# Expert products of the older multiplication, moved ahead of two of four spread batches on TensorE

## What is computed

```python
x = x + _L0_conv_ref(_ln_c(x), conv_w, conv_b)      # conv over [max, mean] of channels, sigmoid, x * scale
t = _to_tokens(x)
router_probs = softmax(ln(t) @ router_w + router_b)
top_p, top_i = top_k(router_probs, 2); top_p /= sum(top_p)
expert_out = einsum('bnd,edc->bnec', ln(t), expert_w) + expert_b
t = t + einsum('bnk,bnkc->bnc', top_p, gathered)     # gathered: expert_out at top_i
```

## Time and profile before

| | us |
|---|---|
| median of 3 runs (lowest, highest) | 1424.98 (1424.57, 1428.08) |
| the profiled execution, its own time | 1424.37 |
| its span in the trace | 1422.6 |
| PE busy | 1310.0 (92%) |
| DVE busy | 1240.8 (87%) |
| POOL busy | 1069.4 (75%) |
| ACT busy | 1054.4 (74%) |

### The profile page before, as it was taken

One profiled execution on the slowest core, in us unless ns is written; L12 is line 12 of the kernel. 1 busy time (PEld: TensorE's weight loads), 2 busy tenths in 40 slices (PEclk: granted clock), 3 DMA queues, 4 the chain that ended last, 5 costly groups with the idle time before them and its releaser, 6 DMA issues.

```text
span 1422.6 us, 33089 instructions
## 1 busy us (share of the span) xinstructions
PE 1310.0 (92%) x11750; PEld 616.6 (43%) x11750; DVE 1240.8 (87%) x1527; ACT 1054.4 (74%) x3949; POOL 1069.4 (75%) x643
## 2 busy tenths in 40 slices
PE   8954999999999999999999999999999988899998
PEld 8853444444444444444444444444444322333332
DVE  5786799979999899988999899988999889987776
ACT  6567898888988898888988899888897334444442
POOL 5334787887788787887887887887888886887765
PEclk9955999999999999999999999999999999999999
DMA  6442466666667667676666666576665555566663
GB/s 220 121 124 81 133 205 195 195 195 203 203 187 219 190 209 211 174 224 195 195 182 216 190 209 204 175 231 198 200 197 156 156 156 156 156 178 185 175 189 117
DMA packets 85845, 259.97 MB, mean 183 GB/s; under 512 B 13744, under 2 KB 13744, under 8 KB 85680
## 3 DMA queue, kind: packets, MB, share of 16 engines
q1 hardware_dynamic: 85680, 257.85, 60.6%
HBM read 206.42 MB, written 51.38 MB: 181 GB/s over the span
## 4 chain that ended last, share of the span: by engine, by line
PE 53%; DVE 24%; issue 12%; POOL 2%; ACT 1%; DVEq 0%; POOLq 0%; ACTq 0%
PE moe L561 31%; DVE gx L703 15%; PE gb L507 8%; PE tm L486 8%; PE tm L500 2%; DVE ge L725 2%; PE moe L555 2%; DVE stats L680 2%; PE tm L546 1%; DVE ot L716 1%; DVE oh L738 1%; PE tm L585 1%; DVE u L788 1%; POOL dl L1235 1%; DVE early_s L680 0%
## 5 line engine op out<-in xcount | busy, mean ns | idle before, releaser
L561 PE MATMUL moe<-gx,wc 128*64 128x448 f32 x3584 | 813.4, 554 | 0.0
L703 DVE TENSOR_TENSOR gx<-gb,xd 128x896 f32<-128x896 f32 x672 | 707.3, 1085 | 85.6 <-PE gb L507 84.8
L1175 POOL TENSOR_TENSOR gx<-gs,xd 128x896 f32<-128x896 f32 x224 | 494.1, 2206 | 250.8 <-ACT gs L990 195.8
L990 ACT ACTIVATE gs<-gb 128x896 f32<-128x896 f32 x224 | 205.3, 916 | 193.9 <-PE gb L507 188.5
L952 ACT ACTIVATE sq<-xct 112x64 f32<-112x64 f32 x1400 | 338.4, 246 | 7.8 <-DVE early_s L690 2.1
L561 PEld LDWEIGHTS moe<-gx,wc 128*64 128x64 f32 x3584 | 217.9, 136 | 195.0 <-issue 162.0
L952 ACT ACTIVATION_READ_ACCUMULATOR sq<-xct 112x1 f32 x1400 | 265.4, 190 | 0.0
L507 PE MATMUL gb<-s,cg 32*128 32x448 f16 x1792 | 186.6, 360 | 64.5 <-DVE gx L703 63.3
L1192 POOL TENSOR_TENSOR tt<-xc,a1s 128x896 f32<-128x896 f32 x112 | 235.5, 2103 | 11.4 <-issue 9.7
L507 PEld LDWEIGHTS gb<-s,cg 32*128 32x128 f16 x1792 | 51.0, 91 | 402.5 <-DVE gx L703 336.4
L486 PE MATMUL tm<-rhs,xa 64*112 64x74 f32 x2800 | 184.6, 272 | 11.8 <-ACT logit_mean L937 8.4
(11 more groups left out here) (93 smaller groups left out, 1091.7 us busy)
## 6 DMA issues: line engine op xcount, KB each, us to landing
xd<-in_x_dram SPq DMA_DIRECT2D x448, 224.0 KB, 4.1
xa<-in_x_dram SPq DMA_DIRECT2D x112, 448.0 KB, 4.5
xc<-in_x_dram SPq DMA_DIRECT2D x112, 448.0 KB, 4.7
out_dram<-ot SPq DMA_DIRECT2D x112, 448.0 KB, 3.6
gx<-in_const_g_dram SPq DMA_DIRECT2D x1, 384.0 KB, 4.7
cf<-in_const_f_dram SPq DMA_DIRECT2D x1, 333.5 KB, 2.8
cf<-in_L_ffn_expert_b_dram SPq DMA_DIRECT2D x12, 1.0 KB
gx<-in_L_ffn_expert_w_dram SPq DMA_DIRECT2D x1, 128.0 KB, 4.5
```

What stands on the lines that cost most here:

```text
L561: last = pe.matmul(moe[b * CH:(b + 1) * CH, c, 0:HALF], wc[:, k * CH:(k + 1) * CH], gx[:, u, b, :], start=False, stop=(k == KT - 1), skip_ ...
L703: dve.tensor_tensor(gx[:, i, :, :], gb[:, 2 * slot:2 * slot + 2, 0:HALF], xd[:, v % 2, :, c * HALF:(c + 1) * HALF], ALU.mult).then_inc(sca ...
L990: act.activation(gs[:, j, :, :], gb[:, 2:4, 0:HALF], ACT.Copy).then_inc(gate_out, 1)
L1175: pool.tensor_tensor(gx[:, ND + j, :, :], gs[:, j, :, :], xd[:, v % 2, :, j * HALF:(j + 1) * HALF], ALU.mult).then_inc(scaled_p, 1)
```

## The change

It moves two calls on PE's queue. In batch 1, E5 of the step before now stands ahead of S1 and SP1, and in batch 3, E2 stands ahead of S4, SP0 and the convolution. No instruction is added or dropped, every wait stays with its instruction, and no other engine's program is changed.

```diff
@@ -605,11 +605,11 @@
                     v = step - LAG
                     cur, ahead = on(r, v), on(r, v + 1)
 
+                    if on(r, v - 1):
+                        experts_of_dve(r, v - 1, 5)
                     if cur:
                         spread_for_dve(r, v, 1)
                         spread_for_pool(r, v, 1)
-                    if on(r, v - 1):
-                        experts_of_dve(r, v - 1, 5)
                     if ahead:
                         turn(r, step, v + 1)
                     if cur:
@@ -626,13 +626,12 @@
                         experts_of_pool(r, v, 0)
 
                     if cur:
+                        experts_of_dve(r, v, 2)
                         spread_for_dve(r, v, 4)
                     if ahead:
                         spread_for_pool(r, v + 1, 0)
                     if Bp and step == 2:
                         convolve(r, A)
-                    if cur:
-                        experts_of_dve(r, v, 2)
                     if ahead:
                         spread_a1(r, step, v + 1, A, Bp)
                     if cur:
```

## The result

The changed kernel takes 1488.31 us, median of 4 runs (1485.12 to 1489.38), beside 1424.81 us for the kernel before: a ratio of 1.0436, 95% interval 1.0413 to 1.0459. It is 63.5 us slower.

A forecast was written before the change was run, and what follows sets the result against it. It took PE's order and whatever holds PE up as the bound beside pass A. The profiled 1424.37 us, plus 80 there, minus 31 afterwards, gave 1473, or 1474 as median; own range 1450 to 1495, stated range 1432 to 1495.

The forecast's parts named there:

- the first stretch: Where pass A runs beside pass C: later spreads stall PE, 13.6 us a round, +80 us in all.
- two chains on ACT: Copies behind the gate copy: s late by 0.80 us, a1 by 0.38, each delaying PE's centring in batches 2 and 4.
- The light step: Step beside pass A with PE busy throughout: 10.92 us, claimed to become 12.10 by stalls of 0.80 and 0.38.
- the sigmoid's 0.7: Step 2: with E2 no longer between convolution and A1, A1 waits some 0.7 us for the sigmoid and handovers.
- The eleven ordinary steps: Steps of a round other than step 2 and the two heavy ones: average 11.25 us, claimed to become 12.17.
- DVE's cover: Batch 1: DVE's gate work or remaining time before S2 hides the 0.80 us later spread, at no cost.
- Rival (1): Only batch 2's stall counts, in the eleven ordinary steps: 52 us less 31, 1445 us; chance 0.13.
- Pass C alone: Last stretch: moved products fill PE's holes, a step falls from 10.23 to 8.96 us; 15 steps, -19 us.
- round 8: Stretch with router work but no pass A: a gain between 0 and 18 us, taken as 12.
- the trap: Router comparison L725 took 7.19 us beside gapless POOL work; its time may shift, left unchanged with 11 us either side.
- the page's version: By the exclusive DVE and GpSimd port lock, shorter steps leave fewer gaps: the stretch without pass A gains 20 us, not 31.
- rival (3): DVE and POOL block each other in more steps, or loads come late in short steps: 1500 us; chance 0.05.

The follow-up runs named there:

- E5: Not a run: PE's expert product call for unit 5, moved in batch 1; against the kernel before, moving only it took 1473.13 us, ratio 1.0335.
- E2 behind the convolution: Changed kernel, but in step 2 E2 stands in its old place after the convolution; 1475.4 us, the middle of two runs.
- the new order from round 8 on: Kernel before, with both moves made only in rounds without pass A; 1413.27 us, ratio 0.9919.
- batch 3 alone: Kernel before, with only E2 moved ahead of S4, SP0 and the convolution, E5 left in place; 1436.02 us, ratio 1.0070.
- the kernels with waits: Three POOL waits for DVE in round 8, added to changed kernel, kernel before, and the new order from round 8 on; 1478.00, 1423.40 and 1406.14 us.
- the copy of parts moved: Changed kernel, with ACT's copy of parts placed after its copy of s instead of ahead of it; 1474.06 us.

## Why the prediction came out as it did

**The mechanism in the first stretch held, step by step.** The claim was that PE's sum doesn't change, that spreads 0.80 later cost DVE nothing, and that two chains on ACT end 0.80 and 0.38 later. Measured were stalls of 0.76 and 0.30, in those two places, 0.14 us behind the ends of those two copies, each shown alone by its own run and the first also from ACT's side. The light step was given as 12.10 and is 11.99; step 2 as 14.9 and is 14.79, with the sigmoid's 0.7 confirmed as 0.68; the heavy steps as +1.0 and are +0.7 (12.93). The eleven ordinary steps average (173.68 - 2 x 12.93 - 14.79) / 11 = 12.09, given as 12.17. A round costs 12.1 where 13.6 was forecast, and the stretch 74.7 where it was 80.

**DVE's cover was as thin as said.** In the light step S2 waits for nothing, so "that last quarter of a microsecond" was enough. Rival (1), that only the stall in batch 2 counts, fell: the one in batch 4 stands in the light step with 0.30, and alone in its own run. DVE's waits absorb a part, as the sum had it: the average ordinary step rose by 0.84 of the 1.07 us.

**Pass C alone**: 8.96 forecast, 8.91 measured, PE busy for all of it. The merged products, the spread behind them, and the window of the step:

```profile
1383.72 2.48 PE L561 MATMUL moe<-gx,wc 128*64 128x448 f32 x12
...
1386.13 0.37 PE L507 MATMUL gb<-s,cg 32*128 32x448 f16 x4
...
1386.43 0.58 PE L500 MATMUL tm<-cg,parts 112*64 112x112 f16 x16
...
1386.43:1395.34 8.91, 8.91 (x78) 3.17 (x74) 7.42 (x8) 4.11 (x5) 7.33 (x5) 1.00 0.73 207
```

The twelve records are E4, EP1 and E5 together, and the transposes follow the full spread of batch 1 by 0.30. That no load would be late in the shorter step, which was only taken to be so, was right: nothing waited there.

**The term that was wrong is round 8.** "Between 0 and 14 x 1.27 = 18, I take 12" was the gain; it was a loss of 9.0. The prediction named the trap, kept the price as it was in the earlier trace rows, and left 11 us either way. It was 21 off. What failed is "I leave it as it is": the blocked instructions became three (24.0 us together, where they need 1.1, 1.1 and 0.6) where one took 7.19 and two were stretched to 2.15 and 2.88, and PE's idle time behind them brought the lower clock three times on twelve records, where it came twice on eight. Why they became more is argued and not shown: POOL has the same work in these 14 steps before and after, 127 to 130 us, while a step in which nothing is blocked can shrink from 10.24 to 8.91 us, which should leave fewer gaps; no run changed that alone. Part of it is chance: the third instruction took 7.83 us here, but 4.79 and 4.81 in two runs whose round 8 is the same (E2 behind the convolution, and the new order from round 8 on). The sentence on the Trainium skill there (SBUF — State Buffer, section "SBUF: two separate sides", an exclusive lock on a shared port pair held for the whole instruction) pointed the right way, and the version of the sum by it, 20 us of gain in the drained stretch where 31 was taken, came nearer to the measured 8. The runs agree with the lock: a DVE instruction with two operands in SBUF comes down to its own time, or towards it, when POOL stops (9.24 to 2.52, 6.91 to 1.09, 1.36 to 0.62). They add that it can lose again at each border of two POOL products, and does not always: once it got through at the first border, in 1.36 us. I should have taken the page's version for the forecast; its 20 was an estimate too. The miss, 1488 against 1474, is this term, 21 us, and 2 us less gain in the last stretch, less the 5 us by which the stalls were overrated and 2 at the ends: 16 us on the profiled executions, 14 on the medians. The total stayed inside the range, though this term did not stay inside its own 11 us.

The sum had the clashes of POOL and DVE in the drained stretch only (rival (3) had them elsewhere, at 0.05). That was wrong too, though it does not show in the changed kernel: with batch 3 alone they cost two steps of each round up to 0.76 us. With both batches these steps are 11.99, as the others, though L729 takes 1.36 and 1.12 ahead of them as well: it seems to have room under PE's longer stalls.

What is not settled: why the same instructions in round 8 take 7.19 us in one execution and 1.36 in another. In both, the DVE instruction was due while POOL was in the short product L1180 (parts); in the run with 1.36 it got through behind it and POOL's next product took 2.60 us and not 1.73, in the other it lost there and twice again. The traces don't show what decides that.

## What to carry to other kernels

Before an instruction is moved ahead of another, follow everyone who waits for the one that is delayed, through the order of their engine: here nobody needed the spread early but one copy, and behind that copy on the same engine stood two others on which the busiest engine waited. A wait that ends at the moment when the waiting engine arrives shows no idle time in a profile and has no slack; the distance from the end of the releaser to the start of the waiter, the same 0.14 us in both batches before and after the change, gives it away. And an order can be right in one stage and wrong in another: the same two moves cost 1.07 us a step beside pass A, cost some 5 us in round 8 and gain 1.33 a step where pass C is alone, so here they belong in the last rounds only.

## What the runs showed of the hardware that was not expected

- A DVE instruction with two SBUF operands can be held for as long as POOL goes on without a gap: 9.24 us for one of about 1.1, through five POOL instructions in a row. A maximum with one operand (L721) kept its 1.07 to 1.09 us in all 64 places, and a product with one operand in PSUM (L702) its 1.04 to 1.09. Which of the two engines gets on at the border of two POOL instructions differs between executions of the same instructions (7.19 us in one, 1.36 in another).
- The times of the kernel before lie in two places: of the 13 runs beside the kernels with waits nine at 1424 to 1426 us, one at 1420 and three near 1417.7. That one blocked instruction makes the difference fits its 6 us, but no run shows it.
- A wait of PE of 8.19 us is followed by about 5 us at the lower clock (0.51 granted). Shorter waits go either way: with the copy of parts moved, step 11 took 14.63 us at a granted clock of 0.88 in one round and 12.94 in another. In both PE waited 1.7 us for DVE before S5, and the twelve records behind it took 4.17 us in the one and 2.48 in the other.
